# Indirect transfers of the mixture-of-experts stage in pairs, each pair begun when the pair ahead of it has landed

## The reference, cut to what matters

```python
logits = t @ Wg                                   # t: (1024, 128) normalized tokens, Wg: (128, 8)
probs = softmax(logits); top_v, top_i = top_k(probs, 2)
top_v = top_v / (sum(top_v) + 1e-8)
for e in range(8):
    h = silu(t @ W1[e]) * (t @ W3[e])             # W1, W3: (128, 512)
    out = out + comb[:, e:e+1] * (h @ W2[e])      # W2: (512, 128); comb is 0 but for the two chosen
```

## Time and profile before

| | us |
|---|---|
| Median of 3 runs | 482.24 |
| Lowest and highest | 481.21, 485.56 |
| The profiled execution | 481.47 |
| Its span (first to last instruction) | 479.4 |
| Around the span (481.47 - 479.4) | 2.1 |

### The profile page before, as it was taken

The page is one execution under the profiler, slowest core; times in us unless marked ns, Lnnn a source line. Parts: engine busy times, 40 slices in busy tenths (PEclk is TensorE's granted clock), DMA queues, the critical chain, the costliest instruction groups (busy, mean ns, idle before and its releaser), DMA issues.

```text
span 479.4 us, 8292 instructions
## 1 busy us (share of the span) xinstructions
PE 389.9 (81%) x2778; PEld 222.9 (47%) x2778; DVE 334.5 (70%) x676; ACT 242.7 (51%) x474; POOL 196.0 (41%) x252
## 2 busy tenths in 40 slices
PE   7768899998688769968986999978797687987950
PEld 3415454664455345435442545533354455754630
DVE  6766594757776899789888997897243765655642
ACT  3615355557345724464667377645583534543530
POOL 5216987362448463570545073625300051051014
PEclk9857999999899999988997899999899989998995
DMA  6672626054016016230242025300300013011112
GB/s 172 141 172 54 145 50 149 0 114 119 0 36 197 1 42 156 75 92 13 78 118 79 2 92 118 89 22 30 100 1 1 12 50 117 24 52 41 34 41 60
DMA packets 44766, 34.67 MB, mean 72 GB/s; under 512 B 5965, under 2 KB 41229, under 8 KB 44429
## 3 DMA queue, kind: packets, MB, share of 16 engines
q1 hardware_dynamic: 43701, 32.03, 25.8%
q0 software_dynamic: 1024, 2.10, 1.5%
HBM read 15.11 MB, written 7.86 MB: 48 GB/s over the span
## 4 chain that ended last, share of the span: by engine, by line
PE 51%; DVE 25%; issue 7%; ACT 6%; SPq 4%; DMA 3%; POOL 2%; another core or an unknown queue 2%; POOLq 0%; DVEq 0%; ACTq 0%
PE p_sc L606 7%; DVE mx L879 6%; PE p_misc L576 6%; PE p_o L638 5%; PE p_o L625 4%; PE p_misc L507 4%; PE p_misc L781 3%; PE p_sc L781 3%; SPq L1430 3%; PE p_o L792 3%; PE p_misc L533 2%; PE p_misc L800 2%; PE p_misc L680 2%; DVE xn L849 2%
## 5 line engine op out<-in xcount | busy, mean ns | idle before, releaser
L879 DVE TENSOR_REDUCE mx<-p_misc 128x1 f32<-128x512 f32 x192 | 122.5, 683 | 27.4 <-PE p_misc L576 26.3
L1190 ACT ACTIVATE probs<-p_sc 128x512 f32<-128x512 f32 x192 | 104.4, 597 | 63.8 <-PE p_sc L606 58.9
L576 PE MATMUL p_misc<-kS,qS 96*128 96x512 f16 x128 | 42.3, 403 | 10.9 <-DVE mx L879 10.9
L1304 POOL TENSOR_SCALAR veps<-meanvar 128x2 f32<-128x2 f32 x16 | 3.9, 246 | 111.0 <-DVE meanvar L835 110.6
L606 PE MATMUL p_sc<-qS,kS 128*128 128x256 f16 x256 | 42.8, 286 | 6.2 <-issue 3.9
L638 PE MATMUL p_o<-probs,v 128*32 128x256 f32 x512 | 42.6, 412 | 0.4 <-issue 0.3
L1346 POOL TENSOR_TENSOR psums<-probs 128x256 f32<-128x256 f32 x32 | 25.3, 792 | 42.2 <-PE p_o L632 38.5
L1368 POOL DMA_INDIRECT probs<-slots_out,kx x16 | 15.1, 946 | 62.9 <-DMA slots_out<-probs 58.6
L1101 DVE TENSOR_TENSOR probs<-probs,p_sc 128x512 f32<-128x512 f32 x30 | 20.6, 685 | 25.7 <-ACT probs L1268 21.4
L625 PE MATMUL p_o<-probs,v 128*64 128x256 f32 x256 | 34.7, 391 | 4.3 <-ACT probs L1190 4.3
L606 PEld LDWEIGHTS p_sc<-qS,kS 128*128 128x128 f16 x256 | 21.7, 101 | 30.2 <-issue 15.3
(11 more groups left out here) (210 smaller groups left out, 767.1 us busy)
## 6 DMA issues: line engine op xcount, KB each, us to landing
region<-kx SPq DMA_DIRECT2D x24, 256.0 KB, 3.9
v<-in_L_ffn_W_dram SPq DMA_DIRECT2D x24, 256.0 KB, 2.7
region<-qx SPq DMA_DIRECT2D x24, 128.0 KB, 3.8
slots_in<-qS SPq DMA_DIRECT2D x2, 960.0 KB, 7.1
slots_out<-probs SPq DMA_DIRECT2D x30, 64.0 KB, 1.5
kS<-kS SPq DMA_DIRECT2D x1, 1664.0 KB
kS<-k_scratch SPq DMA_DIRECT2D x8, 192.0 KB
kS<-slots_in SPq DMA_DIRECT2D x6, 256.0 KB, 3.5
```

The lines of the kernel that those rows point to most:

```text
L576: pe.matmul(ps, q[:, i * P:(i + 1) * P], k, start=True, stop=True).then_inc(full, 1)
L879: dve.tensor_reduce(mx[:, b % 2, i, h:h + 1], ps, AX_X, ALU.max).then_inc(free, 1)
L1190: act.activation(probs[:, h % 8, half * 512:(half + 1) * 512], p_sc[:, half, :], ACT.Exp, scale=(DH0 if layer == 0 else DH1) ** -0.5).then ...
```

## The change

`send` gains a wait ahead of each pair of scatters but the very first: until all pairs ahead of it have landed. For the second half's first pair that count was reached long before. `pick(0)` gains a wait ahead of its second, third and fourth pair until the pair ahead has landed; `pick(1)` is left as it is. One step of `REST` moves: `gT` of the second half's first four tiles from 11.76, between the steps of the tiles, to 13.62, directly ahead of the next `gT`.

```diff
--- before.py
+++ after.py
@@ REST
-        (4.79, 'count', 1), (4.84, 'place', 1), (5.44, 'send', 1), (8.85, 'fetch', 1), (11.76, 'gT', 1, 0),
+        (4.79, 'count', 1), (4.84, 'place', 1), (5.44, 'send', 1), (8.85, 'fetch', 1), (13.62, 'gT', 1, 0),
         (13.86, 'gT', 1, 1), (17.72, 'gT', 1, 2), (18.76, 'gT', 1, 3), (19.42, 'pick', 0), (20.61, 'mix', 0, 0),
@@ send(half)
                 if half == 0:
                     pool.wait_ge(zeroed, 32)
                 for i in range(NT):
+                    if half or i:
+                        pool.wait_ge(sent, 16 * 2 * (half * NT + i))
                     for s in range(2):
                         pool.indirect_dma_start(d_in[half], bass.IndirectOffsetOnAxis(ap=slot_id[:, half, s, i:i + 1], axis=0),
                                                 xe[:, half * NT + i, :], None).then_inc(sent, 16)
@@ pick(half)
                 for i in range(NT):
+                    if half == 0 and i:
+                        pool.wait_ge(picked[i - 1], 16 * 2)
                     for s in range(2):
                         pool.indirect_dma_start(picks[half][:, s, i, :], None, d_out[half],
                                                 bass.IndirectOffsetOnAxis(ap=slot_id[:, half, s, i:i + 1], axis=0)).then_inc(picked[i], 16)
```

## The result

The changed kernel took 466.88 us (median of 4 runs, 465.41 to 470.36), the kernel before, run beside it, 483.85 us (4 runs, 481.21 to 485.56). The ratio is 0.9664, with a 95% interval of 0.9588 to 0.9741: 3.4% faster. The forecast was 467.7 us. The profiled execution has a span of 464.5 us where it was 479.4, 14.9 us less.

A forecast was written before the change was run, and what follows sets the result against it. PE, busy 81% of the span, was taken to set the pace, held up by late signals during POOL's indirect transfers. 16.9 - 1.6 - 0.8 = 14.5 us gained, so 482.24 - 14.5 = 467.7 us; range 464 to 472, with the partly-left case 463 to 479.

The forecast's parts named there:

- Lateness as the thing to be gained: Late PE signals to ACT and DVE while POOL issues eight indirect transfers in a row; all 16.9 us taken as gained.
- the three series: POOL's runs of eight indirect transfers beside PE's work, from 327.59, 387.13 and 423.37: both sends and pick(0); 5.4, 4.1, 7.4 us.
- The rival in which lateness runs on for as long as POOL works through a series: Late signals follow how long POOL works, not open transfers; each run 4.8 us longer, kernel 483 to 494 us; chance 0.14.
- the one in which half of it stays: Two transfers in quick succession still delay PE's signals a little; with half left 475.8 us; chance 0.16.
- the case that the waits buy nothing: Trainium skill's view: each of nine waits that can block costs POOL time without return; answered by the slower rival, chance 0.14.
- A pair has at most two transfers open: Reason for taking all 16.9 us: a pair also lands before 4.3 us, and no late signal showed up to there.
- the 3.3 us of 430.51: ACT's start at 430.51 on PE transposes that ended at 427.18, read as 3.3 us late.
- The pitch of the pairs: Time from pair to pair on POOL with the waits: 4.2 us for scatters, 4.5 for gathers, where it was 2.5.
- PE's wait for the first fetch: fetch(0) on SP starts later, so PE waits for the first half's fetched tiles: cost 1.6 us, bounds 0 and 2.7.
- gT(1,0) next to gT(1,1): Price of the moved step: gT(1,1) needs dn(11)'s PSUM bank, free after DVE's tile 11 result; 0.8 us, bounds 0 and 1.5.
- Hidden with 2 us to spare: keep(7), queued behind fetch(1) on SP, lands at about 407, before DVE's tile 11 result needs it at 408.9; no cost.
- the cover: The 2 us spare at keep(7) behind fetch(1); without it, lateness there would cost microsecond for microsecond.

## Why the prediction was right

- **Lateness as the thing to be gained.** Right, in place and size. The prediction had 5.4, 4.1 and 7.4 us in the three series, 16.9 together. By the rests, pairs in the third series alone gave 7.4 us (and 6.5 when the first two were in pairs already), and pairs in the first two alone gave 8.4 with their costs, where 5.4 - 1.6 + 4.1 - 0.8 = 7.1 was forecast. The rival in which lateness runs on for as long as POOL works through a series, and the one in which half of it stays, both fell: nothing "remote" was left. So did the case that the waits buy nothing.
- **Its reason was half wrong.** "A pair has at most two transfers open" is about as true of the unbroken series, and with work in place of the waits the gain came though the pair hadn't landed. That part was luck. What held is the second half of the sentence: no series shows a late signal before 4.3 us of unbroken transfers. The 4.3 us are where a late signal came in; it was given at 426.74, 3.4 us behind the start, and a pair's last instruction has ended by 2.2. The runs with work in place of waits and with four in a row bear that out.
- **The lateness was read too small.** The prediction took the 3.3 us of 430.51 and the idle times. The signal that ACT got at 434.80 was given at 427.84, 7.0 us before (the rows are shown under the hardware below). The cost was taken from PE's pitch, so the sum doesn't change.
- **The pitch of the pairs** was taken as 4.2 us for scatters, with up to 0.70 for POOL's restart. It measured 3.75: the chain of waits of the changed kernel gives 2.22 to 2.24 us from a scatter's start to its landing for six of the eight pairs, 2.77 and 2.87 for the others, and 0.27 for the restart. The idle time ahead of the pairs was therefore 1.53 us where the prediction looked for 2.0 to 2.3. (An unbroken series took 10.2 us only the first time, 9.9 and 9.7 in the others beside PE.) For gathers 4.5 was taken; 5.2, 3.9 and 4.1 were measured. The first fetch went out at 343.29 (forecast 344.0).
- **PE's wait for the first fetch**, forecast 1.6 us, was smaller. The timeline of PE, compare:

```profile
346.34 0.65 PE L507 MATMUL p_misc<-ident,kS 128*128 128x128 f32 x4 [0.15 <-DMA kS<-slots_in]
...
347.22 0.66 PE L507 MATMUL p_misc<-ident,kS 128*128 128x128 f32 x4 [0.22 <-DMA kS<-slots_in]
```

0.15 and 0.22 us on PE's row; between the two starts lie 0.88 us where transposes take 0.44, so the whole is about 0.6 to 0.8. The net gain of the first series was 4.7 us in place of 3.8.

- **gT(1,0) next to gT(1,1)**, forecast 0.8 us, was larger. The step between tiles 12 and 13 is 2.2 us over the pitch, and two groups of transposes need 0.9, so it cost 1.3. PE waited 0.79 us for DVE's result of tile 11, of the kind and size that was said.
- **"Hidden with 2 us to spare"** was the weakest step, and wrong. The chain of waits of the changed kernel around `fetch(1)` (start us, us, what):

```profile
395.64 2.23 DMA slots_in<-qx,kx
397.87 0.02 issue
397.88 0.37 SPq L1507
...
399.95 3.82 DMA slots_out<-probs
403.77 0.04 DVEq L481
...
403.91 0.24 DVE probs L1112
```

`keep(7)` goes out behind the four fetches and needs 3.82 us to land, where these writes need 1.5 alone. It lands at 403.77, and DVE begins on the result of tile 11 at 403.85, right behind its instruction before. There were 0.1 us to spare, not 2, and the chain of the send now runs straight into the expert loop. In the run with sixteen copies the last pair of the second send waited 3.84 us in place of 2.08, the fetch went out later, and PE's second group of transposes waited 2.49 us for DVE's result of tile 11. That run's rest is 140.9 us, 4.0 above the changed kernel, without anything changed at this place. It looks like the price when the cover is gone, but isn't shown to be: the chain there has `keep(7)` landed at 402.52 and gives no cause for the 1.64 us until DVE starts at 404.16. What held up the landing ahead of the last pair is open too.

By the milestones the gain was 0.9 us above the forecast in the first series, 0.3 below it from tile 5 to 18 (3.0 in place of 4.1 - 0.8), 0.2 below between the two and right in the third. That these nearly cancel is luck: 14.5 us forecast, 14.9 in the profile, and 17.0 between the medians, of which the kernel before's own spread of 4 us allows 2.

## What to carry to other kernels

Breaking a series on an engine that has time to spare was worth 3% here: look in every stretch with indirect transfers for engines that wait on an instruction that has already ended. Here four indirect transfers in a row began to cost and two did not; a wait for the landing and one other instruction of POOL, 1.04 us from transfer to transfer, did equally well. Where POOL has other work due, that work should be the cheapest break, which no run here tried. Where the busy engine isn't running, as at a kernel's end, leave the series unbroken. And when a DMA that a ring of buffers depends on is queued behind large ones, take its landing time from that company, not from its rows elsewhere: 3.82 us here, not 1.5.

## What the runs showed of the hardware

- While POOL issues indirect transfers back to back, signals from PE to ACT and DVE arrive late, from about the fourth transfer on, until the last one has landed (339.16 and 339.13 in the first series). The first late one of the third series was given 3.4 us behind the start (426.74) and came 0.9 us late. The longest idle time on ACT from it is 3.81 us, but the signal itself can be later. The timelines of PE and DVE in the kernel before:

```profile
427.45 0.39 PE L803 MATMUL p_misc<-region,probs 128*128 x4
...
428.28 0.69 DVE L1101 TENSOR_TENSOR probs<-probs,p_sc 128x512 f32<-128x512 f32 x1 [1.65 <-issue]
...
429.05 0.62 PE L792 MATMUL p_o<-ident,probs 128*128 128x128 f32 x4
...
431.13 0.69 DVE L1105 TENSOR_TENSOR probs<-p_o,probs 128x512 f16<-128x512 f32 x1 [2.16 <-issue]
...
431.96 0.72 PE L800 MATMUL p_misc<-region,probs 128*128 x4 [2.28 <-issue]
```

- ACT's copy of 434.80 belongs to the L803 of 427.45, as counting the copies back from the prompt tiles behind it shows. That ended at 427.84, so the signal took 7.0 us. PE wasn't stuck meanwhile: its L792 of 429.05 starts on DVE's result of 428.28, which ended at 428.97.
- Signals from ACT to DVE and from DVE to PE are prompt in the same stretch: ACT's cast of 430.51 took 0.58 us and DVE, on it, started at 431.13; DVE ended at 431.82 and PE, on it, started at 431.96.
- It does not depend on the rows: 32 per transfer stall at least as much as 128. Sixteen plain copies issued by POOL in 8.66 us do nothing of the kind. What in the indirect instruction holds PE's signals up was not found out; no run looked inside it.
- POOL's time for an indirect transfer is nearly fixed: mostly 0.86 us for 32 rows, mostly 0.94 to 0.96 for 128 (now and then up to 1.22).
- A scatter's landing, waited for by POOL, took 1.53 us of idle time ahead of most pairs, and 2.08, 2.55 and 3.84 ahead of the fourth pair of the second send in three profiles; what made these longer is open.
- The same code ahead of the first indirect transfer took 325.4 to 331.3 us in fourteen profiles, which is why single profiles were compared from there.
